# Self attention's head values kept 64 wide, two heads on the column halves, output weights applied per pair

## What is computed

```python
def _mha(s, t, kv_w, q_w, o_w, o_b, mask):
    k, v = jnp.split(s @ kv_w, 2, axis=-1)
    q = t @ q_w
    k, v, q = (_heads(k), _heads(v), _heads(q))          # 16 heads of 64
    scores = jnp.einsum('bhqd,bhkd->bhqk', q, k) * D ** (-0.5)
    scores = jnp.where(mask[:, None] == 0, -1e9, scores)
    attn = jax.nn.softmax(scores, axis=-1)
    o = jnp.einsum('bhqk,bhkd->bhqd', attn, v)
    return o.transpose(0, 2, 1, 3).reshape(...) @ o_w + o_b
...
tn = _ln(t, norm_g, norm_b); t = _mha(tn, tn, skv, sq, sow, sob, tgt_mask) + t    # self attention
tn = _ln(t, norm_g, norm_b); t = _mha(src, tn, ckv, cq, cow, cob, src_mask) + t   # cross attention, 77 keys
tn = _ln(t, pg, pb);         t = t + relu(tn @ w1 + b1) @ w2 + b2
```

## Time and profile before

| | |
|---|---|
| median of 3 runs | 1139.71 us |
| the profiled execution's own time | 1137.97 us |
| its span in the profile | 1136.1 us |
| TensorE matmul busy | 1043.2 us (92%) |
| ScalarE busy | 773.5 us (68%) |
| VectorE busy | 751.3 us (66%) |
| GpSimd busy | 385.2 us (34%) |
| chain that ended last: TensorE | 83% of the span |
| one steady layer (s0 58.7, s1 35.4, x0 27.3, x1 49.7) | 171.1 us |

### The profile page before, as it was taken

The page is one execution under the profiler, slowest core; times in us unless marked ns, Lnnn a source line. Parts: engine busy times, 40 slices in busy tenths (PEclk is TensorE's granted clock), DMA queues, the critical chain, the costliest instruction groups (busy, mean ns, idle before and its releaser), DMA issues.

```text
span 1136.1 us, 21080 instructions
## 1 busy us (share of the span) xinstructions
PE 1043.2 (92%) x5374; PEld 659.5 (58%) x5374; DVE 751.3 (66%) x4546; ACT 773.5 (68%) x3453; POOL 385.2 (34%) x398
## 2 busy tenths in 40 slices
PE   5469999999999999999999999999999999999874
PEld 3346655656655656655656655666655666655532
DVE  2736578856678855678765678765678765678634
ACT  2128689856689856689856589856589856589821
POOL 2003344322344322354322354322354323354310
PEclk9659999999999999999999999999999999999987
DMA  8320110000410000310000410000410000000000
GB/s 240 50 70 1 51 33 1 1 1 11 115 33 2 1 1 2 121 35 1 2 1 1 121 37 2 1 1 2 121 36 1 2 1 1 20 1 1 1 0 19
DMA packets 37263, 32.45 MB, mean 29 GB/s; under 512 B 10768, under 2 KB 32528, under 8 KB 35984
## 3 DMA queue, kind: packets, MB, share of 16 engines
q1 hardware_dynamic: 37136, 31.03, 9.8%
HBM read 30.49 MB, written 0.52 MB: 27 GB/s over the span
## 4 chain that ended last, share of the span: by engine, by line
PE 83%; DVE 10%; issue 3%; ACT 2%; DVEq 1%; DMA 0%; SPq 0%
PE sum L856 23%; PE S L826 21%; PE T L836 11%; PE W L740 4%; PE W L682 4%; PE W L746 4%; PE W L669 2%; PE W L720 2%; PE W L699 2%; DVE Pb L1192 2%; PE W L735 2%; DVE XN L1045 1%; PE W L651 1%; PE W L660 1%; DVE stats L1034 1%
## 5 line engine op out<-in xcount | busy, mean ns | idle before, releaser
L986 ACT ACTIVATE Pb<-Pb,mn 128x128 f32<-128x128 f32 (+1 forms) x1536 | 560.9, 371 | 65.0 <-DVE mn L1192 65.0
L547 POOL TENSOR_TENSOR Pb<-Pb,rsum 128x512 f32<-128x512 f32 (+2 forms) x336 | 325.1, 969 | 600.6 <-DVE rsum L1200 600.1
L986 ACT ACTIVATION_READ_ACCUMULATOR Pb<-Pb,mn 128x1 f32 x1536 | 294.8, 192 | 0.0
L836 PEld LDWEIGHTS T<-ident,Pb 128*128 128x128 f32 (+2 forms) x1296 | 163.7, 147 | 153.9 <-issue 114.8
L1192 DVE CUSTOM_DVE_ANT_0 Pb<-S,late_bias 128x128 f32<-128x128 f32 x768 | 175.5, 285 | 110.5 <-PE S L826 109.8
L826 PE MATMUL S<-GV,XT 128*128 128x512 f32 x384 | 197.2, 600 | 1.4 <-DVE mn L1192 0.8
L836 PE MATMUL T<-ident,Pb 128*128 128x128 f32 (+2 forms) x1296 | 197.4, 273 | 0.0
L856 PE MATMUL sum<-PT,GV 128*128 128x512 f32 x384 | 192.4, 593 | 0.0
L1209 DVE COPY PT<-T 128x512 f32<-128x512 f32 (+1 forms) x240 | 157.3, 656 | 43.6 <-PE T L836 42.1
L1192 DVE CUSTOM_DVE_ANT_0 Pb<-S,cross_bias 128x77 f32<-128x77 f32 x768 | 132.4, 233 | 42.8 <-PE S L826 38.8
L856 PE MATMUL sum<-PT,Vc 128*128 128x512 f32 (+2 forms) x264 | 134.5, 599 | 0.0
(11 more groups left out here) (136 smaller groups left out, 1071.8 us busy)
## 6 DMA issues: line engine op xcount, KB each, us to landing
sakv<-in_L_xattn_sa_kv SPq DMA_DIRECT2D x6, 1024.0 KB, 5.3
caow<-in_L_xattn_ca_ow SPq DMA_DIRECT2D x132, 32.0 KB, 2.3
saq<-in_L_xattn_sa_q SPq DMA_DIRECT2D x6, 512.0 KB, 6.1
caq<-in_L_xattn_ca_q SPq DMA_DIRECT2D x6, 512.0 KB, 8.1
cakv<-in_L_xattn_ca_kv SPq DMA_DIRECT2D x6, 512.0 KB, 9.4
saow<-in_L_xattn_sa_ow SPq DMA_DIRECT2D x6, 512.0 KB, 4.2
w<-in_L_xattn_ff_w SPq DMA_DIRECT2D x12, 256.0 KB, 3.1
GV<-in_mask_BxSxS_ik SPq DMA_DIRECT2D x1, 2048.0 KB, 10.1
```

What stands on the lines that cost most here:

```text
L547: nc.gpsimd.tensor_tensor(rows, rows, r, ALU.mult).then_inc(sem(f"{unit.name}_weights"), 1)
L836: last = nc.tensor.transpose(T_ps[n % 2][0:k1 - k0, t * P:(t + 1) * P], Pb[:, n % SLOTS, k0:k1], ident[:])
L986: last = nc.scalar.activation(Pb[:, s, t * w:(t + 1) * w], Pb[:, s, t * w:(t + 1) * w], ACT.Exp, bias=mn[:, s, t:t + 1], scale=-1.0, accum ...
```

## The change

Job "V" and its copies go from the fast path. Job "v" now makes the values with the keys on the partitions (`v_own`, 128 keys x 512 for 8 heads), in one matmul with the features stationary. A new job "o" takes a pair of heads: for each a matmul with 64 columns of `v_own` stationary and `PT` streamed, into the partitions 0 to 63 and 64 to 127 of one bank of the ring. The result is copied into `o_pair` by VectorE (even pairs) or ScalarE (odd pairs). `attend` becomes one matmul per pair, `saow` of the pair stationary and `o_pair` streamed, 8 for a phase in place of 16. "o" stands 1 and 3 ticks after the start of the next group, for the last group of a phase both pairs 1 tick after the end; `attend` 2 ticks later. The steps after self attention move by up to two ticks, and `saow` is loaded once `oT` of both batches is made.

```diff
-SELF1_AT = (24, 25, 26, 26, 27, 34)
-SELF0_AT = (18, 18, 20, 26, 28, 32)
+SELF1_AT = (24, 25, 26, 27)
+SELF0_AT = (18, 18, 26, 28)
...
-AFTER_S0 = (2, 4, 6, 6, 7, 10)
-AFTER_S1 = (2, 3, 4, 4, 5, 6)
+AFTER_S0 = (3, 4, 5, 6, 7, 8)
+AFTER_S1 = (3, 4, 5, 6, 7, 8)
...
         for g, group in enumerate(self.groups):
+            if not group.cross and not wide:
+                first = self.end[group.j, group.phase % 4] if group.last else self.tick_of[(g + 1) * TB]
+                for i in range(TB // 2):
+                    fill = first + 1 + (0 if group.last else 2 * i)
+                    self.jobs[fill].append(("o", group.j, group.b, 2 * group.index + i))
+                    self.attend[fill + 2].append((g, i))
+                continue
...
-            kv, keys, values = when[3 * i:3 * i + 3]
+            kv, keys = when[2 * i:2 * i + 2]
             self.jobs[at + kv] += [("k", j, b, i), ("v", j, b, i)]
             self.jobs[at + keys] += [("G", j, b, i, 0), ("G", j, b, i, 1)]
-            self.jobs[at + values] += [("V", j, b, i, 0), ("V", j, b, i, 1)]
...
 def by_vector(event):
-    return event[0] in ON_VECTOR
+    return event[0] in ON_VECTOR or event[0] == "o" and event[3] % 2 == 0
...
-                        emptied(FAST, ("V", j, 1, 1, 1), 0)
+                        sp.wait_ge(sem("fast_oT"), 4 * j + 2)
                         load_o(j + 1)
...
+                    elif what == "v":
+                        last = nc.tensor.matmul(w[:], XT[:, b * T + KEYS:(b + 1) * T], sakv[:, c0 + i * T:c0 + (i + 1) * T],
+                                                start=True, stop=True)
...
+                elif what == "o":
+                    b, p = event[2:4]
+                    g = unit.first_group[4 * j + b] + p // 2
+                    made(ring, [("v", j, b, p // TB)], l, fills)
+                    if p % 2 == 0:
+                        for i in range(2):
+                            pe.wait_ge(sem(f"{unit.name}_turned_sb{i}"), (g + 1) * (TB // 2))
+                    for h in range(2):
+                        c = (2 * p + h) % 8 * D
+                        last = nc.tensor.matmul(w[half(h), :], v_own[:, b, p // TB, c:c + D], PT[:, g % 2, p % 2 * 2 + h, :],
+                                                start=True, stop=True)
...
+                    if not group.cross and not unit.wide:
+                        p = 2 * group.index + blk
+                        if group.first and blk == 0:
+                            pe.wait_ge(sem("saow_in"), 16 * (j + 1))
+                            if group.phase > 0:
+                                pe.wait_ge(sem(f"{unit.name}_oT"), group.phase)
+                        made(ring, [("o", j, b, p)], l)
+                        mm = nc.tensor.matmul(sum_ps[:], saow[:, p, :], o_pair[:, p % 2, :], start=(p == 0), stop=(p == NPAIR - 1))
+                        if blk == 1:
+                            mm.then_inc(sem(f"{unit.name}_attended"), 1)
+                        return
...
+                elif what == "o":
+                    last = nc.scalar.activation(o_pair[:, event[3] % 2, :], w[:], ACT.Copy)
...
-                    last = nc.vector.tensor_copy(vT[:], w[:])
+                    last = nc.vector.tensor_copy(vT[:] if unit.wide else v_own[:, event[2], event[3], :], w[:])
+                elif what == "o":
+                    last = nc.vector.tensor_copy(o_pair[:, event[3] % 2, :], w[:])
```

More of the change, by code:

```diff
@@ L217, in place @@
             self.early[1 + 4 * b].append(("xn", 0, b, 0))
-        self.self_operands(0, 0, 1, (0, 2, 3, 4, 6, 7))
+        self.self_operands(0, 0, 1, (0, 2, 4, 6))
         for j in range(self.layers):
@@ L314, in build @@
         full_bias = GV[:, 4:12, :]
+        v_own = GV[:, 8:12, :].rearrange("p (b i) n -> p b i n", b=B)
+        o_pair = sb("o_pair", [P, 2, T])
         Gc = sb("Gc", [P, 2, B, H * M])
@@ L382, in half, with transposed_read @@
             return slice(h % 2 * D, h % 2 * D + D)
+        def transposed_read(unit, g, l):
+            group = unit.groups[g]
+            if group.cross or unit.wide:
+                return f"{unit.name}_attended", l * len(unit.groups) + g + 1
+            pair = ("o", group.j, group.b, 2 * group.index + 1)
+            return unit.ring.full(pair), unit.ring.value(pair, l)
         block = ctx.enter_context(nc.Block())
@@ L705, in work @@
                     pe.wait_ge(sem("saow_in"), 16 * n_in)
[L706 to L723, removed]
+                    p, h = divmod(event[3], 2)
+                    made(ring, [("v", j, b, p)], l, fills)
+                    for i in range(TB):
+                        last = nc.tensor.matmul(w[:, i * P:(i + 1) * P], vT[half(h), i * P:(i + 1) * P],
+                                                saow[half(h), p, :], start=True, stop=True)
+                elif what == "o":
[9 more added lines that the diff above has]
+                                                start=True, stop=True)
                 elif what == "fin":
@@ L849, in attend @@
                         if not group.cross:
-                            values = [("V", j, b, group.index // 2, h) for h in range(2)]
-                            made(ring, [("V", j, b, group.index)] if unit.wide else values, l)
+                            made(ring, [("V", j, b, group.index)], l)
                         elif group.first:
@@ L994, in evacuate_turned @@
                     if gr >= 2 and qt < 2:
-                        act.wait_ge(sem(f"{unit.name}_attended"), l * len(unit.groups) + gr - 1)
+                        name, value = transposed_read(unit, gr - 2, l)
+                        act.wait_ge(sem(name), value)
                     nc.scalar.activation(PT[:, gr % 2, 0:group.blocks, qt * P:(qt + 1) * P],
@@ L1109, in work @@
                 elif what == "v":
-                    last = nc.vector.tensor_copy(vT[:], w[:])
+                    last = nc.vector.tensor_copy(vT[:] if unit.wide else v_own[:, event[2], event[3], :], w[:])
+                elif what == "o":
+                    last = nc.vector.tensor_copy(o_pair[:, event[3] % 2, :], w[:])
                 elif what == "V":
[L1112 to L1117, removed]
+                    last = nc.vector.tensor_copy(V[:, 4 + event[3] % 4, :, :], tiles(w[:]))
                 else:
@@ L1207, in evacuate_turned @@
                     if gr >= 2 and qt < 2:
-                        dve.wait_ge(sem(f"{unit.name}_attended"), l * len(unit.groups) + gr - 1)
+                        name, value = transposed_read(unit, gr - 2, l)
+                        dve.wait_ge(sem(name), value)
                     nc.vector.tensor_copy(PT[:, gr % 2, 0:group.blocks, qt * P:(qt + 1) * P],
```

## The result

| | before | after |
|---|---|---|
| median | 1139.26 us (4 runs, 1136.59 to 1141.12) | 1156.95 us (4 runs, 1152.96 to 1158.37) |
| ratio | | 1.0151 [1.0119, 1.0184] |
| profiled execution, its span | 1137.97, 1136.1 us | 1152.96, 1151.1 us |

What follows compares the result with a forecast made beforehand. TensorE, busy 92% of the span, was taken to bound the kernel. Its work -2.4, the steps after s1 -5 and new waits +3 gave -4.4 us, on the median 1135.3 us, range 1122 to 1152.

Steps and rivals of the forecast that it cites:

- TensorE, part by part: TensorE's work: "V" -31.0, "v" -0.9, `attend` -82.4, "o" +82.4, changes of array division +29.5; sum -2.4 us.
- Rivals 1 and 2: Column halves not at once: 1217.7 us, chance 0.10 (partial overlap 1176.5, 0.06); crossings only 0.2 us: 1122 us, chance 0.08.
- The steps after s1: In x0, most of 1.7 us waiting goes, 0.4 to 0.9 comes before x1's scores: -0.9 us a layer, -5 in six.
- The other engines: VectorE unchanged, ScalarE 28 us busier; `o_pair` copies covered by TensorE's other work in s0 and s1, costed at nothing.
- New waits: Waits of other kinds in s0 and s1: 0 to +1 us a layer, +3 us taken for all.
- The windows: Phase times: s0 within 0.5 us of 58.7, s1 +1 to 1.5, x0 -0.5 to -1.5, x1 about -1.2.
- Rival 3: Cover fails: ScalarE lags, TensorE waits for `o_pair`, "xn" or transposes; some +14 on the sum, 1149 us, chance 0.14.

Runs made afterwards that it cites:

- the kernel with both edits: Kernel after with even o copies on ScalarE, odd on VectorE, last group's pairs a tick earlier, s1's others in adjacent ticks, old steps after self attention: 1140.25 us, 1.0013.
- e5: Kernel after with the o copies swapped, even pairs on ScalarE and odd pairs on VectorE: 1150.38 us, 1.0106.
- e8: Kernel before with only the steps after s1 moved as in the change: 1149.39 us, 1.0093.
- e6: Kernel after with the last group's pairs a tick earlier, s1's other pairs in adjacent ticks, and the old steps after self attention: 1149.0 us, 1.0085.

## Why the prediction was wrong

**TensorE, part by part: right.** Busy time is 1040.0 us in the kernel with both edits against 1043.2 before, -3.2 where I forecast -2.4 (in after 1044.8, part of it at the lower clock). Pairs at once and a crossing of 0.35 us are shown by the two timelines, with and without the crossing. Rivals 1 and 2 are out. The Trainium skill, TensorE: Matmul & The Clock Gate, Part 3 on packing, section The mechanism, says that weight loads overlap with running matmuls only when their row groups differ; the runs here don't bear that out for column halves, whose 64 column loads share all rows and lay under the pair's first matmuls (0.20 us from 692.20): four instructions took 2.42 - 0.43 - 0.78 = 1.21 us with the crossing. The same section also names a background weight buffer that a load may go to ahead of running matmuls; no run here tells whether that is what is seen.

**"The steps after s1": wrong, and the largest part.** I forecast -0.9 us a layer. I had the place right (scores of x1 behind ScalarE's copy of "xn") and the size wrong: 0.4 to 0.9 us of waiting forecast, 1.8 to 2.0 measured. I counted the transposes of "xn" and the copy itself, 0.77, but not what stands ahead of that copy in ScalarE's queue: four exponentials, 711.96 to 713.35, which wait for a maximum that waits behind the normalised rows on VectorE. The normalised rows stand in the earlier trace rows; the exponentials were one view further, in ScalarE's timeline. I had looked at the time between "fin" and "xn" on TensorE, 6.8 us against 4.6, and not walked the other two queues through that tick. Shown both ways: the edit alone costs the kernel before +10.2 us, and taking it back gives the kernel with swapped copies -10.1. Per layer it is +0.8 us at full clock in the kernel before, where I had -0.9 (in the changed kernel, where "xn" waits only 0.2, +0.5: 171.7 us a layer with the new steps, 171.2 with the old). Of the +10.2, the longer stops are 0.8 us in five layers and 1.5 in the last, 5.6. The rest, some 4.6, I put down to the lower clock, by the phases of one execution; its mean clock, 0.966 against 0.970 in the profile of before, gives the same as an estimate (0.004 x 1148 us, if TensorE bounds throughout). No run holds the clock fixed, so this share is argued and not shown. The clock was in no term of my sum, since the earlier trace rows show it full.

**"The other engines" at nothing: wrong by one place.** For the copies of `o_pair` I set 1.3 us of cover in s0 against a copy of 0.69 and asked what is queued *behind* the copy, not ahead of it. In one tick of five layers the normalised rows (1.1 us) stand ahead of it. Shown by giving the even pairs to ScalarE: -6.6 us, and s0 is 1.5 us shorter. ScalarE's busy time rose by 22 us and not by 28.

**New waits, +3:** about right for what stays: 3.5 us of the transposes in the kernel with both edits. With the -2.4 of TensorE that gives +1.1, which is its measured distance from before (1140.25 - 1139.18 = 1.1). That it fits to a tenth is luck: the interval of that run reaches from 0 to 3 us.

**The windows.** s0 within 0.5 us of 58.7: held (58.7), but by luck: a wait of 1.3 to 1.5 us and a phase otherwise shorter by 1.7 cancel. s1 +1 to 1.5: +1.2. x1 about -1.2: -1.1. x0 -0.5 to -1.5: +2.5, the failed step (x1's 1.1 us only move into x0, as the edit to the steps alone shows: x1 -1.1, x0 +1.9). Together with e5's 6.6, e8's 10.2 and the 1.1 left, the parts give 17.9 of the 17.7 measured; since clock falls come and go between executions, this sum is no closer than a few us.

**Rival 3** was the one that came: TensorE waits for `o_pair` and for "xn". I had given it 0.14 and +14 on the sum (1149), for a microsecond in each phase of self attention and one behind "xn"; by these words it is 12 + 6 = 18, and the 14 is not worked out. The waits in s0 and s1 are fewer than that, the one behind "xn" is double, and a lower clock goes with it. My reason against it, that TensorE gets slower there and ScalarE's lag shrinks, spoke of ScalarE's average load; the two waits come from the order within a queue, which no busy share shows.

## What to carry over

When a step is moved to another tick, walk each engine's queue through that tick, what stands ahead of the moved instruction included: a copy of 0.77 us was worth 1.8 because four exponentials stood before it. When stops of TensorE grow or move in a kernel that is otherwise dense, look at the granted clock of every run before its microseconds are put down to an edit. And weigh arithmetic that is folded into other work against the changes of division that unfolding brings: here 82 us less `attend`, 82 more "o" and 84 crossings against 24 came out even within 0.3%.

## What the runs showed of the hardware

- Two fp32 matmuls with 64 columns each and 128 rows streamed ran at once on the column halves: four instructions of 512 columns took 1.21 us, crossing included, where two full ones took 0.86. So a crossing there and back cost 0.35 us, against 0.39 for the row halves.
- The granted clock fell from 1.00 to 0.50 around the end of a stop of TensorE within otherwise dense work: of 1.75 to 2.0 us before the scores of x1, of 1.7 before the cG of x1 (after at 752 us, and the kernel with both edits at 405), of 3.1 near the end, and once (e6, at 190) behind two stops of 1.0 and 0.6. The fall began between 0.8 us before the stop's end and 1.6 us behind it. Most such stops had none: in after a fall came with one of the six before the scores of x1 and with one of the five before the cG. In the profile of before no stretch between 100 and 1088 us shows a fall, though it too stops 1.6 us in x1, five times, and once 3.1 us at 1067. Between executions of one program, a mean clock of 0.966 in place of 0.972 went with 5.2 us. So what ties the fall to these orders of work is read from where it comes in the traces and not shown by a run of its own, and why it comes in one layer and not in the next is open.
- 36 crossings fewer gave 4 us in after and cost 7 in the kernel with both edits: in s0 the bunched copies cost more than the crossings. In s1 18 went without any gain in s1 and x0 together: the 1.0 us a phase came back as one late maximum and what follows it (TensorE waits for maxima 10.3 us in place of 7.5 between 100 and 1080 us).
